# Cross and causal attention units in a mixed order, transposed scores 15 tiles behind

## The reference

```
x = x + tanh(g_xattn) * cross(layernorm(x), ctx, ctx)    # softmax(q k^T / sqrt(8)) v, 16 heads
y = layernorm(x)
q, k = rope(y) @ Wq^T + bq, rope(y) @ Wk^T + bk ;  v = y @ Wv^T + bv
a = causal softmax attention(q, k, v) @ Wo^T + bo
x1 = layernorm(y + a) * w1 + b1
gates = softmax(x1 @ Wg^T + bg), the two largest of 8 kept
out = x + tanh(g_ffn) * (layernorm(x1 + sum of the gated experts) * w2 + b2)
```

## Time and profile before

| | us |
|---|---|
| median of three runs | 520.43 (519.47 to 521.97) |
| profiled execution | 522.93 |
| its span | 521.1 |
| TensorE busy | 448.9 (86%) |
| VectorE busy | 385.2 (74%) |
| GpSimd busy | 323.7 (62%) |
| ScalarE busy | 278.6 (53%) |

### The profile page before, as it was taken

The page is one execution under the profiler, slowest core; times in us unless marked ns, Lnnn a source line. Parts: engine busy times, 40 slices in busy tenths (PEclk is TensorE's granted clock), DMA queues, the critical chain, the costliest instruction groups (busy, mean ns, idle before and its releaser), DMA issues.

```text
span 521.1 us, 15905 instructions
## 1 busy us (share of the span) xinstructions
PE 448.9 (86%) x5728; PEld 280.0 (54%) x5728; DVE 385.2 (74%) x1191; ACT 278.6 (53%) x693; POOL 323.7 (62%) x702
## 2 busy tenths in 40 slices
PE   0369788778888899999999999999789999999983
PEld 0134444444444456666666666666447666666652
DVE  6377878787786777767777777773269899999981
ACT  1126656666565665666656666666444554554530
POOL 1445654565468898887888878621044766667654
PEclk9999979888797999999999999999879999999995
DMA  4565775556343434344343443420000000000000
GB/s 108 127 170 132 183 173 128 125 141 152 94 108 95 103 91 98 86 106 110 96 98 85 105 115 93 98 70 10 3 0 11 12 20 23 10 22 11 23 20 20
DMA packets 88333, 42.70 MB, mean 82 GB/s; under 512 B 16312, under 2 KB 88128, under 8 KB 88256
## 3 DMA queue, kind: packets, MB, share of 16 engines
q1 hardware_dynamic: 79040, 39.59, 30.8%
q10 hardware_dynamic: 9216, 2.10, 2.0%
HBM read 5.75 MB, written 2.10 MB: 15 GB/s over the span
## 4 chain that ended last, share of the span: by engine, by line
PE 32%; DVE 20%; POOL 17%; issue 6%; ACT 2%; POOLq 0%; ACTq 0%; DVEq 0%
PE u_bank L421 6%; DVE z_acc L922 5%; PE s_bank L374 4%; PE s_bank L364 4%; POOL xn_all L238 4%; PE u_bank L773 2%; POOL rstd L233 2%; PE u_bank L434 2%; PE s_bank L752 2%; DVE nm L599 2%; POOL rc L256 2%; PE st_bank L752 2%; PE t_bank L346 2%; POOL z_rstd_ L650 2%; DVE stats L555 1%
## 5 line engine op out<-in xcount | busy, mean ns | idle before, releaser
L599 DVE TENSOR_REDUCE nm<-s_bank 128x4 f32<-128x512 f32 x256 | 173.1, 684 | 73.5 <-PE s_bank L374 71.7
L499 ACT ACTIVATE pt<-st_bank 128x512 f32<-128x512 f32 x256 | 150.0, 598 | 102.6 <-PE st_bank L374 60.4
L374 PE MATMUL s_bank<-qk 64*128 64x128 bf16 x1024 | 105.7, 231 | 11.3 <-DVE nm L599 7.7
L421 PE MATMUL u_bank<-pt,vaug 128*32 128x128 f32 x2048 | 113.8, 296 | 0.0
L374 PE MATMUL st_bank<-qk 64*128 64x128 bf16 x1024 | 106.4, 227 | 0.0
L374 PEld LDWEIGHTS s_bank<-qk 64*128 64x128 bf16 x1024 | 70.7, 99 | 39.2 <-issue 27.7
L374 PEld LDWEIGHTS st_bank<-qk 64*128 64x128 bf16 x1024 | 71.4, 98 | 0.4
L421 PEld LDWEIGHTS u_bank<-pt,vaug 128*32 128x32 f32 x2048 | 41.4, 111 | 29.0 <-issue 4.1
L364 PE MATMUL s_bank<-mqk,esel 64*128 64x256 bf16 x256 | 49.7, 274 | 0.4 <-ACT pt L499 0.4
L364 PE MATMUL st_bank<-mkq,esel 64*128 64x256 bf16 x256 | 49.7, 274 | 0.0
L280 POOL TENSOR_TENSOR part<-r,part 128x512 bf16<-128x512 f32 x32 | 37.1, 1159 | 2.7
(11 more groups left out here) (118 smaller groups left out, 904.3 us busy)
## 6 DMA issues: line engine op xcount, KB each, us to landing
qk<-part SPq DMA_DIRECT2D x224, 128.0 KB, 2.6
x_all<-x SPq DMA_DIRECT2D x16, 128.0 KB, 2.6
c_all<-ctx_in SPq DMA_DIRECT2D x16, 128.0 KB, 2.8
qk<-qrow SPq DMA_DIRECT2D x32, 64.0 KB, 2.1
qk<-mts ACTq DMA_DIRECT2D x64, 32.0 KB, 2.6
out<-z_o SPq DMA_DIRECT2D x16, 128.0 KB, 1.8
ewt<-exp_t SPq DMA_DIRECT2D x1, 512.0 KB
qk<-krow SPq DMA_DIRECT2D x4, 64.0 KB, 2.0
```

Of the source, the lines that this page charges most:

```text
L374: return pe.matmul(bank[:, j * P:(j + 1) * P], k if keys_first else q, q if keys_first else k, start=not masked, stop=True, skip_group_che ...
L421: ins = pe.matmul(u_bank[b][32 * j:32 * j + 32, r * P:(r + 1) * P], v, pt[m % 4][:, j, :], start=half == 0, stop=half == 1, skip_group_che ...
L499: act.activation(pt[m % 4][:, :, :].rearrange("k j q -> k (j q)"), st_bank[m % 2][:, :], ACT.Exp).then_inc(ex, 1)
L599: dve.tensor_reduce(nm[q % 2][:, first:first + HEADS], s_bank[n % 2][:, :].rearrange("q (j k) -> q j k", j=HEADS), AX_X, ALU.max, negate=T ...
```

## The change

The two kinds of unit are put in one list `ORDER`: seven cross units, then nine times a causal and a cross unit in turn, then seven causal units. Counts of semaphores, buffers and groups are taken from this list (`xs`, `ys`, `group`) in place of u and GROUPS; the semaphore of normalised rows is two now, one for each kind. `LAG` goes from 13 to 15, and with it `AV_LAG`, `U_COPY`, `U_TURN`, `U_NORM` and `U_ADD`, by two slots each. There are five value buffers, and `ve` and `rstd` are doubled. The later constants are loaded from slot -2 on, three at a time, `esel` in slot 0, biases in slot 1, the row and column constants by ScalarE ahead of everything else, and they are awaited at slot 4. Which step stands at which t, and that a causal unit's normalisation and rotation run three units ahead and all else two, stays.

```diff
@@ -24,25 +24,31 @@
 TILES = G * 4
 HEADS = 4
 RING = 4
+V_RING = 5
 PARTS = 3
 SLOTS = 7
 Q_PART = (0, 1, 0, 1, 0, 1, 2)
 K_PART = (0, 1, 2, 0, 1, 2, 0)
 STACK = SLOTS + 1
-LAG = 13
+LAG = 15
 AV_LAG = LAG + 2
 U_COPY = AV_LAG + 4
 U_TURN = U_COPY + 1
 U_NORM = U_COPY + 2
 U_ADD = U_COPY + 3
 UNITS = 2 * GROUPS
+FIRST_X = 7
+ORDER = [("x", g) for g in range(FIRST_X)]
+for g in range(GROUPS - FIRST_X):
+    ORDER += [("y", g), ("x", FIRST_X + g)]
+ORDER += [("y", g) for g in range(GROUPS - FIRST_X, GROUPS)]
 SEQS = UNITS * G
 LAST_TILE = UNITS * TILES
 FIRST_SLOT = -2 * TILES
 END_SLOT = LAST_TILE + AV_LAG + 8
 AHEAD = 4
 EARLY, LATER = 4, 28
-LATE_STEP = 9
+LATE_STEP = 4
...
-        vaug = [sb(f"vaug{i}", [P, G, H, 48]) for i in range(RING)]
+        vaug = [sb(f"vaug{i}", [P, G, H, 48]) for i in range(V_RING)]
         stats = [sb(f"stats{i}", [P, G, 6]) for i in range(2)]; mv = [sb(f"mv{i}", [P, G, 2]) for i in range(2)]
-        ve = sb("ve", [P, G]); rstd = sb("rstd", [P, G])
+        ve = [sb(f"ve{i}", [P, G]) for i in range(2)]; rstd = [sb(f"rstd{i}", [P, G]) for i in range(2)]
...
         def in_x(u):
-            return 0 <= u < GROUPS
+            return 0 <= u < UNITS and ORDER[u][0] == "x"
 
         def in_y(u):
-            return GROUPS <= u < UNITS
+            return 0 <= u < UNITS and ORDER[u][0] == "y"
+
+        def xs(u):
+            return sum(kind == "x" for kind, _ in ORDER[:u + 1])
+
+        def ys(u):
+            return sum(kind == "y" for kind, _ in ORDER[:u + 1])
+
+        def group(u):
+            return ORDER[u][1]
...
         def pair(t, u):
-            g = u % GROUPS
+            g = group(u)
             return t[:, g * G:(g + 1) * G, :]
 
         def one(t, q):
-            return t[:, q % B, :]
+            return t[:, group(q // G) * G + q % G, :]
 
         def stacked(u):
             return 16 * STACK * (u // RING + 1)
 
         def high_parts(u):
-            return u + 1 if u < GROUPS else 2 * (u + 1) - GROUPS
+            return xs(u) + 2 * ys(u)
...
+        def later_constants(eng, first, end):
+            for dst, src in ((mqk, mask_qk), (mkq, mask_kq), (wq, wq_t), (wk, wk_t), (wv, wv_t), (cost, cos_t),
+                             (sint, sin_t), (wo, wo_t), (gwt, gate_t), (ewt, exp_t), (ebs, exp_b))[first:end]:
+                eng.dma_start(dst[:, :], src).then_inc(c_late, 16)
+
+        def later_rows(eng):
+            for dst, src in ((bvb, bv), (bob, bo), (gbb, gate_b), (l1w, ln1w), (l1b, ln1b), (l2w, ln2w), (l2b, ln2b)):
+                row(eng, dst[:, :], src, c_late)
+            for dst, src in ((l1wc, ln1w), (l1bc, ln1b)):
+                eng.dma_start(dst[:, :], src.rearrange("(n o) -> n o", o=1)).then_inc(c_late, 16)
...
-                if 1 <= s <= 6:
-                    later_constants(sp, 4 * (s - 1), min(4 * s, 20))
-                if s == 5:
+                if -2 <= s <= 2:
+                    later_constants(sp, 3 * (s + 2), 3 * (s + 3))
+                if s == 0:
                     for half in range(2):
                         for block in range(2):
                             sp.dma_start(esel[64 * half:64 * half + 64, block, :],
                                          identb[64 * block:64 * block + 64, :]).then_inc(c_late, 16)
-                if s == 6:
+                if s == 1:
                     for dst, src in ((bqs, bq), (bks, bk)):
...
             def normalised(u):
+                i = u % 2
                 pool.wait_ge(stat, (u + 1) * 4)
-                if in_x(u - 1):
-                    pool.wait_ge(ln, u * G)
+                if u >= 2:
+                    pool.wait_ge(lnx if in_x(u - 2) else lny, G * (xs(u - 2) if in_x(u - 2) else ys(u - 2)))
                 by = 1.0 / SCALE ** 2 if in_x(u) else 1.0
-                pool.tensor_scalar(ve[:, :], mv[u % 2][:, :, 1], by, EPS * by, ALU.mult, ALU.add).then_inc(rstd_s, 1)
+                pool.tensor_scalar(ve[i][:, :], mv[i][:, :, 1], by, EPS * by, ALU.mult, ALU.add).then_inc(rstd_s, 1)
                 pool.wait_ge(rstd_s, u * 2 + 1)
-                pool.tensor_tensor(rstd[:, :], ve[:, :], mhalf[:, :], ALU.pow).then_inc(rstd_s, 1)
-                pool.wait_ge(rstd_s, u * 2 + 2)
+                pool.tensor_tensor(rstd[i][:, :], ve[i][:, :], mhalf[:, :], ALU.pow).then_inc(rstd_s, 1)
                 if in_x(u):
                     return
-                for b in range(G):
-                    pool.tensor_scalar(one(xn2_all, u * G + b), one(x_all, u * G + b), mv[u % 2][:, b, 0:1],
-                                       rstd[:, b:b + 1], ALU.subtract, ALU.mult).then_inc(ln, 1)
+                pool.wait_ge(rstd_s, u * 2 + 2)
+                for b in range(G):
...
             def values(u):
-                act.wait_ge(x_in[u % AHEAD], 32 * (u // AHEAD + 1))
-                if u >= RING:
-                    act.wait_ge(av_s, (u - RING + 1) * TILES)
-                act.activation(vaug[u % RING][:, :, :, 16:16 + D],
+                loaded(act, u)
+                if u >= V_RING:
+                    act.wait_ge(av_s, (u - V_RING + 1) * TILES)
+                act.activation(vaug[u % V_RING][:, :, :, 16:16 + D],
                                pair(c_all, u).rearrange("k b (h d) -> k b h d", d=D), ACT.Copy).then_inc(vx, 1)
 
...
         def _(act):
+            later_rows(act)
             act.wait_ge(c_dma, 16 * EARLY)
             act.activation(tg[:, :], gates[:, :], ACT.Tanh).then_inc(c_tanh, 1)
...
-            for i in range(RING):
+            for i in range(V_RING):
                 dve.memset(vaug[i][:, :, :, :], 0.0).then_inc(c_low, 1)
             dve.wait_ge(c_zero, ROW_ZEROS)
-            dve.wait_ge(c_low, RING)
+            dve.wait_ge(c_low, V_RING)
             for half in range(2):
```

More of the change, by code:

```diff
@@ L162, in row, with load_inputs @@
                          ).then_inc(semaphore, 16)
-        def load_inputs(sp, u):
-            if u >= AHEAD:
-                sp.wait_ge(x_in[u % AHEAD], 32 * (u // AHEAD))
+        def load_inputs(sp, g):
+            mine = slice(g * G, (g + 1) * G)
+            if g >= AHEAD:
+                sp.wait_ge(x_in[g % AHEAD], 32 * (g // AHEAD))
             for dst, src in ((x_all, x), (c_all, ctx_in)):
-                sp.dma_start(pair(dst, u), pair(src.rearrange("b s d -> s b d"), u)).then_inc(x_in[u % AHEAD], 16)
@@ L170, in later_constants @@
[L170 to L184, removed]
-                    sp.dma_start(dst[:, :], src.rearrange("(n o) -> n o", o=1)).then_inc(c_late, 16)
+                sp.dma_start(dst[:, mine, :], src.rearrange("b s d -> s b d")[:, mine, :]).then_inc(x_in[g % AHEAD], 16)
@@ L284, in max_split @@
                 b = q % 2
-                to = mst[q >= B][b][:, :].rearrange("q (half p hs) -> q half p hs", half=2, hs=HS)
+                to = mst[in_y(q // G)][b][:, :].rearrange("q (half p hs) -> q half p hs", half=2, hs=HS)
                 whole = nm[b][:, :].rearrange("q (half hs) -> q half hs", half=2)
@@ L310, in pool_attention @@
                 q = seq_at(n, U_ADD)
-                if q is not None and q < B:
+                if q is not None and in_x(q // G):
                     add_residual(q)
@@ L419, in av @@
                     h = 2 * (HEADS * r + j) + half
-                    v = vaug[u % RING][:, b, h, 16 * (1 - half):16 * (1 - half) + 32]
+                    v = vaug[u % V_RING][:, b, h, 16 * (1 - half):16 * (1 - half) + 32]
                     ins = pe.matmul(u_bank[b][32 * j:32 * j + 32, r * P:(r + 1) * P], v, pt[m % 4][:, j, :],
@@ L428, in transpose_max @@
                     pe.wait_ge(mts_s, q)
-                pe.transpose(m_bank_b[:, 0:P], mst[q >= B][q % 2][:, :], idb[:, :]).then_inc(mt, 1)
+                pe.transpose(m_bank_b[:, 0:P], mst[in_y(q // G)][q % 2][:, :], idb[:, :]).then_inc(mt, 1)
             def transpose_u(q):
@@ L470, in high_part @@
                 else:
[L471 removed]
+                    act.wait_ge(proj, ys(u))
                 if u >= 2:
@@ L548, in statistics @@
                 if in_x(u):
-                    dve.wait_ge(x_in[u % AHEAD], 32 * (u // AHEAD + 1))
+                    loaded(dve, u)
                 else:
-                    dve.wait_ge(res, (u - GROUPS + 1) * G)
+                    dve.wait_ge(res, (group(u) + 1) * G)
                 if u >= 2:
-                    dve.wait_ge(ln, (u - 1) * G)
+                    dve.wait_ge(lnx if in_x(u - 2) else lny, G * (xs(u - 2) if in_x(u - 2) else ys(u - 2)))
                 for b in range(G):
@@ L560, in normalised @@
             def normalised(u):
+                i = group(u)
                 dve.wait_ge(rstd_s, u * 2 + 2)
[L562 to L563 removed]
+                if i >= 2:
+                    dve.wait_ge(tr, ORDER.index(("x", i - 2)) + 1)
                 for b in range(G):
[L565 removed]
+                    dve.tensor_scalar(xp[i % 2][:, b, :].rearrange("q (x hs) -> q x hs", hs=HS),
```

(2 more changed lines are left out.)

67 lines of the change are left out of this document (35 added, 32 removed).

## The result

The changed kernel takes 546.83 us (544.95 to 547.07, 4 runs) against 519.95 before: ratio 1.0481, interval 1.044 to 1.0521. I had forecast 528.5 with a range of 514 to 537. The sign was right, the size was not: +26.9 us instead of +8.1. Spans of the profiled executions: 545.1 against 521.1, +24.0.

The account below looks back on a forecast made before the run. Causal slots were taken as bound by TensorE, cross slots as losing time in hand-overs. Start 1.6, SyncE 1.2, lag 1.6 and 3.7 from unit 4 on gave +8.1 on the median 520.4: 528.5 us, range 514 to 537.

Parts of the forecast that it names:

- Start: Head of the kernel: the fifth value buffer's memset delays TensorE's first transpose, +1.6 us.
- ScalarE had only waited for loads in that time, so I take 0; the bounds are 0 and 2: Head: ScalarE's nine early loads, 4 us of issuing, cost nothing, or up to 2 if their traffic delays input loads.
- SyncE: SyncE's queue: constants ahead of the operand stacks make unit 4's first score late, +1.2 us (0 to 3).
- Lag 15: Two more tiles after the last maximum, +2.0, less 0.4 at the head: +1.6 us (1 to 2.5).
- -0.4 for the head: First units: two tiles at the head go without transposed scores and values, 0.2 us a tile saved.
- only have to live longer: Value buffers and stacks under the longer lag: they need only longer life, which the fifth buffer pays for.
- Alternation: Mixed part: a causal and cross pair costs 21.7 us against 21.4; from unit 4 on +3.7 us.
- A causal slot: 10.9 and 0.1 for the late split, 11.0: Mixed causal slots: 10.9 us as before plus 0.1 (0 to 0.75) waiting for GpSimd's late split of maxima.
- a cross slot: 9.7 where the clock holds: Mixed cross slots: 9.7 us at held clock, 11.2 where it dips; six of nine dipped, 10.7 on average.
- The clock holds: Rival, chance 0.28: full causal slots keep TensorE at 2.4 GHz through cross slots; pairs 20.45 us, total 517.
- GpSimd and SyncE bind: Rival, chance 0.14: each cross slot 11.2 us, each causal slot 0.4 more, SyncE 2 later; total 538 us.

Follow-up runs that it names:

- e_rows_later: The changed kernel with ScalarE's nine row and column loads issued in slot -1 behind the high part instead of first of all; 545.58 us.
- e_lag15: The kernel before in its own order, with lag 15 and five value buffers alone, constants loaded as before; 523.73 us, ratio 1.0027.
- e_before_fill3: The kernel before with useless matrix products in TensorE's waits of slots that prepare a cross unit, from slot 3 on only; 519.58 us, ratio 0.9949.
- e_mixed_lag13: The changed kernel with lag 13 again, all else kept; 543.76 us, ratio 1.0423 to the kernel before.
- e_norm_early: The changed kernel with VectorE's normalisation of a finished sequence one slot earlier, at t = 2, 6 instead of 3, 7; 538.39 us.
- e_lag15_norm_early: The kernel before in its own order with lag 15, five value buffers and VectorE's normalisation one slot earlier; 530.8 us, ratio 1.0149.
- e_fill: The changed kernel with useless matrix products in TensorE's waits of the slots that prepare a cross unit; 539.51 us, ratio 1.0336.

## Why the prediction was wrong

Of the 15.9 us between the +8.1 forecast and the +24.0 of the spans, 2.3 lie before the first maximum, 1.3 from there to unit 4, 11.8 from unit 4 to the last maximum and 0.4 behind it. Of the 11.8, 10.3 are in the nine pairs (205.6 against 195.3).

*Start, +1.6 predicted, +3.9 measured.* The memset was right to 0.1. "ScalarE had only waited for loads in that time, so I take 0; the bounds are 0 and 2" failed: with these loads in front, SyncE's issues and landings were slower, 2.5 us at the first maximum (e_rows_later).

*SyncE, +1.2 predicted, +2.5 measured in unit 3's slot.* The mechanism was right. TensorE waited 3.2 us, and 2.2 came back when the queue was freed; I had allowed up to 3. Unit 3 itself was ready sooner than the 9.55 of before, at 8.9, which made the stacks later against it.

*Lag 15, +1.6 predicted.* Its tail is +2.4 in the spans (+2.2 in e_lag15). The -0.4 for the head was read from a slot at half clock. The earlier trace rows shows 1.00 for unit 2, but the first clock record of the trace is at 49 us, and before it eight value products take this:

```profile
43.56 0.66 PE L421 MATMUL u_bank<-pt,vaug 128*32 128x128 f32 x8
```

In e_before_fill3 nearly all of them take 0.43 us in unit 2 and the slot is 9.12 instead of 10.60. So unit 2's slot is 0.2 longer than unit 1's by its tiles, not 1.7, and two tiles of it are worth next to nothing. The step that failed is the sentence that the buffers "only have to live longer". I had noted that `U_NORM` hangs on the lag, and did not follow where it would stand on VectorE. In causal slots that is +0.41 each in e_lag15 and 0.45 to 0.5 from e_mixed_lag13 to the changed kernel, some 7 us over sixteen. That the place of the normalisation decides is shown where nothing else was moved: causal slots between causal ones went from 11.31 to 10.65 (e_norm_early, e_lag15_norm_early), mixed ones only from 11.34 to 11.12.

*Alternation, pairs 21.7 predicted, 22.85 measured.* The step "A causal slot: 10.9 and 0.1 for the late split, 11.0" failed: 12.10. 0.45 of it is the lag. The rest, 0.75, is nearly all half clock (e_fill gives back 0.63), and I had put half-clock stretches into cross slots alone, since before they were found there alone. e_fill gives 8.4 us for the clock in the pairs. The sum was nevertheless forecast well, 1.0 a pair for the half clock against 0.93 by e_fill; only its place was wrong. What the change added by the clock is smaller: 0.93 against the 0.67 of before is 2.4 us over nine, and the two runs with products, 7.3 us gained in the one kernel and 2.4 in the other, give 5.

The step "a cross slot: 9.7 where the clock holds" failed too: 10.41, which is 6.4 us over nine. The average came to 10.75 against 10.7 forecast, by luck of terms: the undisturbed slot was longer, the disturbed one shorter (10.99, not 11.2). GpSimd's second split ends 8.0 us after its first begins, not 7.3: the doubled `rstd` removed the wait of 0.58, but two waits for VectorE's statistics, 0.45 and 0.26, stand in its place. The first split began 0.66 before the slot and not 0.45 into it, so the second was done 7.4 us into the slot, even before the 7.8 forecast. But TensorE, which was to want it at 7.4, stood there after 5.85 us and waited 1.6 and not 0.4. With lag 13 it comes there after 6.9 us and waits 1.0 (e_mixed_lag13), so the longer lag let it run ahead, into the wait; by which step was not tested.

*The rivals.* "The clock holds", and with it the Trainium skill's rule that activity releases the throttle ("TensorE: Matmul & The Clock Gate", Part 1) as I applied it, did not come true: between full causal slots only four of nine cross slots kept 1.00. The rule itself fits e_fill, where activity inside the holes held 1.00. "GpSimd and SyncE bind" came nearest with 538, and both its waits are there, 1.6 us for the split and 3.2 for the stacks; it had no term for the moved normalisation, for the half clock in causal slots or for the nine loads.

What stays open: of the 1.9 us that a mixed pair costs above an own-order pair in the end, at least 0.7 is GpSimd's train. VectorE's share, and that of the one tile in eight whose two kinds of score belong to units of different kind, were not measured apart.

## What to carry to other kernels

A constant that sets a delay moves every step that is counted from it; look at what each then stands in front of in its engine's queue, for each kind of slot. Where a short slot with holes alternates with one that TensorE fills, most of the half clock that the holes start is paid in the full one (0.63 of 0.93 us a pair here). Useless products can hold the clock, but look at each place whether the awaited thing is ready before they are done: then they are the wait. Compare undisturbed slots with undisturbed ones before the clock is blamed. Loads issued early on an idle engine can still delay those that the head waits for: nine cost 2.5 us here.

## What was not expected of the hardware

Products without use in TensorE's waits were worth 7.3 us in the changed kernel (546.8 to 539.5) and, from slot 3 on, 2.4 us in the kernel before: at 0.98 mean clock instead of 0.95, more instructions took less time. And nine small loads (six of 64 KB and one of 4 KB, rows spread over 128 partitions, and two columns of 0.5 KB) more than doubled the landing time of four 64 KB DMAs on another queue, 4.3 us instead of 2.0.
